# Gate logits from the transposed residual, and the dispatched rows written one step later, in a fused graph layer and mixture of experts

## What is computed

```python
# first layer
xn  = layernorm(x)
agg = eps * xn + einsum('bnm,bmd->bnd', adj, xn)
h   = silu(rmsnorm(agg @ W1 + b1) * rms_w)          # 512 features
x1  = x + h @ W2 + b2
# second layer, on u = layernorm(x1)
logits = u @ gate_w + gate_b                        # 16 experts
vals, idx = top_k(logits, 2);  w = softmax(vals)
expert_out[e] = relu(u @ w1[e] + b1[e]) @ w2[e] + b2[e]
y   = u + sum_k w[k] * expert_out[idx[k]]
out = x1 + layernorm(y) * gamma + beta
```

## Time and profile before

| | |
|---|---|
| median of 3 runs | 963.91 us (963.61 to 967.44) |
| the profiled execution | 964.82 us, its span 963.0 us |
| PE busy | 771.8 us (80%) |
| DVE busy | 598.9 us (62%) |
| ACT busy | 552.4 us (57%) |
| POOL busy | 508.1 us (53%) |
| HBM | 145 GB/s over the span |
| costliest group | L495 POOL, 256 indirect DMAs, 251.1 us busy |

### The profile page before, as it was taken

One profiled execution on the slowest core, in us unless ns is written; L12 is line 12 of the kernel. 1 busy time (PEld: TensorE's weight loads), 2 busy tenths in 40 slices (PEclk: granted clock), 3 DMA queues, 4 the chain that ended last, 5 costly groups with the idle time before them and its releaser, 6 DMA issues. The chain is left out here.

```text
span 963.0 us, 15762 instructions
## 1 busy us (share of the span) xinstructions
PE 771.8 (80%) x3649; PEld 506.7 (53%) x3650; DVE 598.9 (62%) x2164; ACT 552.4 (57%) x1123; POOL 508.1 (53%) x539
## 2 busy tenths in 40 slices
PE   5999999999999989858789999999986888772000
PEld 3455555555555445436567777777765666552000
DVE  2678787777777757764656665677755454443233
ACT  2799999999999969863223334545443433333121
POOL 2005666666666656666103555455455555557774
PEclk9999999999999989986989999999999978876555
DMA  5354444444344411142656777777775756553222
GB/s 158 112 209 144 150 148 147 150 146 149 133 146 148 139 54 48 43 112 80 180 149 168 184 187 196 200 218 211 215 194 166 193 145 169 168 143 110 73 82 79
DMA packets 136676, 140.76 MB, mean 146 GB/s; under 512 B 18323, under 2 KB 112291, under 8 KB 136358
## 3 DMA queue, kind: packets, MB, share of 16 engines
q1 hardware_dynamic: 117750, 102.67, 35.4%
q0 software_dynamic: 16384, 34.11, 12.6%
q10 hardware_dynamic: 2480, 3.34, 1.0%
HBM read 74.57 MB, written 65.49 MB: 145 GB/s over the span
## 5 line engine op out<-in xcount | busy, mean ns | idle before, releaser
L495 POOL DMA_INDIRECT dispatched<-rows,slot_i x256 | 251.1, 981 | 207.0 <-issue 132.0
L518 POOL DMA_INDIRECT work<-results,place x184 | 180.5, 981 | 188.1 <-issue 69.6
L825 ACT ACTIVATE hid<-bank,wts 128x256 f32<-128x256 f32 x286 | 120.1, 471 | 272.3 <-PE bank L665 270.6
L665 PE MATMUL bank<-tut,wts 128*128 128x256 f32 x572 | 162.1, 409 | 42.4 <-DVE tut L1221 37.4
L680 PE MATMUL bank<-w_all,hid 128*128 x1144 | 175.2, 299 | 0.0
L1243 DVE SCALAR_TENSOR_TENSOR tout<-bank,gate,tin 128x128 f32<-128x128 f32 x274 | 83.5, 347 | 124.5 <-PE bank L680 119.1
L680 PEld LDWEIGHTS bank<-w_all,hid 128*128 128x128 f32 x1144 | 147.2, 201 | 18.4 <-issue 2.7
L665 PEld LDWEIGHTS bank<-tut,wts 128*128 128x128 f32 x572 | 105.0, 205 | 56.1 <-DVE tut L1221 40.6
L544 PE MATMUL bank<-agg,w_sb 128*128 128x512 f32 x256 | 124.9, 610 | 0.0
L559 PE MATMUL bank<-work,w_sb 128*128 128x512 f32 x256 | 118.7, 607 | 3.8 <-ACT work L810 3.8
L518 POOL DMA_INDIRECT rows<-results,place x72 | 69.6, 967 | 49.8 <-issue 26.9
(11 more groups left out here) (190 smaller groups left out, 1031.4 us busy)
## 6 DMA issues: line engine op xcount, KB each, us to landing
tin<-dispatched SPq DMA_DIRECT2D x143, 132.0 KB, 2.8
wts<-in_w_exp SPq DMA_DIRECT2D x143, 129.0 KB
results<-tout SPq DMA_DIRECT2D x26, 704.0 KB, 3.1
results<-tout SPq DMA_DIRECT2D x137, 128.0 KB, 2.0
xs<-in_x SPq DMA_DIRECT2D x32, 256.0 KB, 2.7
adj_sb<-in_adj_t SPq DMA_DIRECT2D x32, 256.0 KB, 3.0
out<-agg SPq DMA_DIRECT2D x32, 256.0 KB, 2.7
dispatched<-rows,slot_i POOLq DMA_INDIRECT x256
```

The costliest lines, as they stand in the source:

```text
L495: nc.gpsimd.indirect_dma_start(dispatched, bass.IndirectOffsetOnAxis(slot_i[:, k, n:n + 1], 0), rows[:, k, n // TOPK, n % TOPK, :], None). ...
L518: nc.gpsimd.indirect_dma_start(moe_of(g)[:, n // TOPK, n % TOPK, :], None, results, bass.IndirectOffsetOnAxis(place[:, g, n:n + 1], 0)).th ...
L665: last = nc.tensor.matmul(hid_ps[n % 2][:, c * TILE:(c + 1) * TILE], wts[:, k, c * P:(c + 1) * P], tut[:, n % 2, :], start=True, stop=True)
L825: last = nc.scalar.activation(hid[:, n % 2, c, :], hid_ps[n % 2][:, c * TILE:(c + 1) * TILE], ACT.Relu, bias=wts[:, k, F + c:F + c + 1], s ...
```

## The change

- x is passed a second time, transposed (features, graphs, nodes), and SP loads it in each step for group t (256 KB) into `x1_t`, a ring of three.
- The second layer's output is no longer taken out of PSUM by ACT (o_t). DVE adds it, b2 and the transposed x in one operation into `x1_t`, after adj plus eps and ahead of the slots. PE transposes `x1_t` back, and DVE copies the result to x1 (it no longer adds).
- The logits come from `x1_t` with gate weights of which the mean over features was taken off (a matmul with ones and one DVE operation, once); the scale 1/sigma and the bias are put on by four small DVE operations in place of one. PE's transposes of rows and ACT's copy ut are gone.
- ACT writes `rows` of group t-3 instead of t-2, in the same place of its step. The gap goes through a tile of its own, `gaps`; `slot_i` has six buffers instead of three.
- In the last steps relu of tile 0 comes ahead of step 33 on ACT.

```diff
@@ sync, step
+                g = t
+                if has(i, g):
+                    if g >= RING:
+                        sp.wait_ge(lg_done, count(i, g - RING + 1))
+                    sp.dma_start(x1_t[:, g % RING].rearrange("p (j n) -> p j n", n=P),
+                                 x_t[:, bass.ds(count(i, g, GB), GB), :]).then_inc(xt_in[g % RING], 16)
@@ tensor, step
-                g = t - 2
-                if has(i, g):
-                    k = g % RING
-                    pe.wait_ge(u_done, count(i, g + 1))
-                    if g >= 1:
-                        pe.wait_ge(slote_done, count(i, g))
-                    for j in range(GB):
-                        last = nc.tensor.transpose(misc_ps[:, j * P:(j + 1) * P], rows[:, k, j, 0, 0:D],
-                                                   ident[:])
-                    last.then_inc(ut_done, 1)
                 g = t - 1
                 if has(i, g):
-                    pe.wait_ge(ot_out, count(i, g + 1))
+                    pe.wait_ge(x1t_done, count(i, g + 1))
                     for j in range(GB):
-                        last = nc.tensor.transpose(out_ps[:, j * D:(j + 1) * D], o_t[:, j * P:(j + 1) * P], ident[:])
+                        last = nc.tensor.transpose(out_ps[:, j * D:(j + 1) * D],
+                                                   x1_t[:, g % RING, j * P:(j + 1) * P], ident[:])
                     last.then_inc(out_done, 1)
...
                 g = t - 2
                 if has(i, g):
-                    pe.wait_ge(ut_out, count(i, g + 1))
+                    if g >= 1:
+                        pe.wait_ge(slote_done, count(i, g))
                     for j in range(GB):
-                        last = nc.tensor.matmul(misc_ps[:, j * E:(j + 1) * E], ut[:, j * P:(j + 1) * P],
-                                                gw2_sb[:], start=True, stop=True)
+                        last = nc.tensor.matmul(misc_ps[:, (GB + j) * E:(GB + j + 1) * E],
+                                                x1_t[:, g % RING, j * P:(j + 1) * P], gw2_sb[:],
+                                                start=True, stop=True)
                     last.then_inc(lg_done, 1)
@@ scalar, step
-                g = t - 2
+                g = t - 3
                 if has(i, g):
                     k = g % RING
...
                     last.then_inc(u_done, 1)
-                g = t - 1
-                if has(i, g):
-                    act.wait_ge(ot_done, count(i, g + 1))
-                    nc.scalar.activation(o_t[:], out_ps[:, :], ACT.Identity, bias=b2_sb[:, 0:1]).then_inc(ot_out, 1)
...
-                if ahead_of_ut is not None:
-                    ahead_of_ut()
-                g = t - 2
-                if has(i, g):
-                    act.wait_ge(ut_done, count(i, g + 1))
-                    nc.scalar.activation(ut[:], misc_ps[:, :], ACT.Copy).then_inc(ut_out, 1)
...
             step(None, NG)
-            step(None, NG + 1, ahead_of_ut=lambda: tile_step(None, 0))
+            tile_step(None, 0)
+            step(None, NG + 1)
@@ vector
+            def centre_gate():
+                dve.wait_ge(gsum_mm, 1)
+                dve.wait_ge(gw2_made, 1)
+                nc.vector.scalar_tensor_tensor(out=gw2_sb[:], in0=misc_ps[:, 2 * GB * E:(2 * GB + 1) * E],
+                                               scalar=-2.0 / D, in1=gw2_sb[:], op0=ALU.mult, op1=ALU.add)\
+                    .then_inc(gw2_made, 1)
@@ vector, step: routing of t-3
-                    nc.vector.tensor_tensor(lgs[:], misc_ps[:, 0:GB * E].rearrange("p (j e) -> p j e", e=E),
-                                            gb_sb[:, :].unsqueeze(1).broadcast_to([P, GB, E]), ALU.add)\
-                        .then_inc(lg_out, 1)
+                    dve.nop(nofuse=True)
+                    for j in range(GB):
+                        last = nc.vector.scalar_tensor_tensor(
+                            out=lgs[:, j, :], in0=misc_ps[:, (GB + j) * E:(GB + j + 1) * E],
+                            scalar=rs[:, 1, k, j:j + 1], in1=gb_sb[:], op0=ALU.mult, op1=ALU.add)
+                    last.then_inc(lg_out, 1)
@@ vector, step: between adj plus eps and the slots
+                g = t - 1
+                if has(i, g):
+                    k = g % RING
+                    dve.wait_ge(xt_in[k], count(i, g // RING + 1, 16, 1))
+                    dve.wait_ge(ot_done, count(i, g + 1))
+                    nc.vector.scalar_tensor_tensor(out=x1_t[:, k], in0=out_ps[:, :], scalar=b2_sb[:, 0:1],
+                                                   in1=x1_t[:, k], op0=ALU.add, op1=ALU.add).then_inc(x1t_done, 1)
@@ vector, step: slots, residual
-                    nc.vector.tensor_copy(slot_i[:, k, :], slot_f[:]).then_inc(slot_done, 1)
+                    if g >= 2 * RING:
+                        dve.wait_ge(u_done, count(i, g - RING + 1))
+                    nc.vector.tensor_copy(slot_i[:, g % (2 * RING), :], slot_f[:]).then_inc(slot_done, 1)
...
-                    nc.vector.tensor_tensor(x1, out_ps[:, :].rearrange("p (b d) -> p b d", d=D), x1,
-                                            ALU.add).then_inc(x1_done, 1)
+                    nc.vector.tensor_copy(x1, out_ps[:, :].rearrange("p (b d) -> p b d", d=D)).then_inc(x1_done, 1)
```

More of the change, by code:

```diff
@@ L45, with gnn_moe @@
 RMS_EPS = 1e-6
-def gnn_moe(nc, x, adj_t, eps, w1, b1, rms_w, w2, b2, gate_w, gate_b, w_exp, w2_exp, b2_exp, gamma, beta, out):
+def gnn_moe(nc, x, x_t, adj_t, eps, w1, b1, rms_w, w2, b2, gate_w, gate_b, w_exp, w2_exp, b2_exp, gamma, beta, out):
     fp32, bf16, i32, u32 = mybir.dt.float32, mybir.dt.bfloat16, mybir.dt.int32, mybir.dt.uint32
@@ L84, in gnn_moe @@
         b2_sb = sb("b2_sb", [P, 1])
-        o_t = sb("o_t", [P, GB * P])
+        x1_t = sb("x1_t", [P, RING, GB * P])
         b2e_sb = sb("b2e_sb", [E, D])
@@ L214, in gnn_moe @@
         ot_done = sem("ot_done")
-        ot_out = sem("ot_out")
+        x1t_done = sem("x1t_done")
+        xt_in = ring_of("xt_in", RING)
+        gsum_mm = sem("gsum_mm")
         h_done = sem("h_done")
@@ L495, in step @@
                         nc.gpsimd.indirect_dma_start(
-                            dispatched, bass.IndirectOffsetOnAxis(slot_i[:, k, n:n + 1], 0),
+                            dispatched, bass.IndirectOffsetOnAxis(slot_i[:, g % (2 * RING), n:n + 1], 0),
                             rows[:, k, n // TOPK, n % TOPK, :], None).then_inc(scattered[k], 16)
@@ L554, in step @@
                         pe.wait_ge(mid_in, 16 * 4)
+                        nc.tensor.matmul(misc_ps[:, 2 * GB * E:(2 * GB + 1) * E], ones_f[:], gw_sb[:],
+                                         start=True, stop=True).then_inc(gsum_mm, 1)
                     pe.wait_ge(s_done, count(i, HC * (g + 1), 1, RING * HC))
@@ L732, in _, with step @@
             act.wait_ge(eps_in, 32)
-            def step(i, t, ahead_of_ut=None):
+            def step(i, t):
                 g = t + 3
@@ L790, in step @@
                     last.then_inc(xn_done, 1)
-                if ahead_of_ut is not None:
-                    ahead_of_ut()
-                g = t - 2
-                if has(i, g):
-                    act.wait_ge(ut_done, count(i, g + 1))
-                    nc.scalar.activation(ut[:], misc_ps[:, :], ACT.Copy).then_inc(ut_out, 1)
                 def half_gap(g):
                     act.wait_ge(gap_done, count(i, g + 1))
-                    gap = rows[:, g % RING, :, :, D + 1:D + 2].rearrange("p j c o -> p (j c o)")
-                    nc.scalar.activation(gap, gap, ACT.Tanh, scale=0.5).then_inc(tanh_done, 1)
+                    nc.scalar.activation(rows[:, g % RING, :, :, D + 1:D + 2].rearrange("p j c o -> p (j c o)"),
+                                         gaps[:, g % 2].rearrange("p j c -> p (j c)"), ACT.Tanh, scale=0.5)\
+                        .then_inc(tanh_done, 1)
                 if not has(i, t) and has(i, t - 3):
@@ L1028, in step @@
                 if i is None and t == 2:
+                    centre_gate()
                     dve.wait_ge(b2_cut, 1)
@@ L1359 @@
         "x": a["x"].transpose(1, 0, 2),
+        "x_t": a["x"].transpose(2, 0, 1),
         "adj_t": a["adj"].transpose(2, 0, 1),
```

17 lines of the change are left out of this document (8 added, 9 removed).

## The result

The changed kernel is slower: 972.15 us (median of 22 runs, 968.25 to 983.53) against 965.99 for the kernel before in the same comparison (22 runs, 960.47 to 970.41). The ratio is 1.0075, with a 95% interval of 1.0059 to 1.0090. The forecast was a ratio of 0.996 and a range of 951 to 969; sign and range were both missed. Ratios leave out the few runs in which the chip was in a slower state; medians are over all runs.

What follows compares the result with a forecast made beforehand. The TensorE-VectorE ring (11.83 us) and GpSimd's slower scatter (about 12.2) were taken to pace the first stage. Terms: +4.8 to group 31's second layer, -8.2 at the stage's end, -0.5 after, -3.9; median 960.0 us, range 951 to 969.

Steps and rivals of the forecast that it cites:

- the ring: First stage: second layer, VectorE's slots to product, then TensorE's mean square and gate logits close each step in 11.83 us.
- The rival that the operation doesn't lengthen the steps: First stage: the ring shrinks elsewhere, steps stay at 12.17 us, total 951.6; chance 0.10.
- The size of the ring: 0.61 a step: Regular step: new VectorE operation 0.66 less 0.05, second layer ending before the rank matmul; ring grows to 12.44 us.
- Loop: Steps 3 to 24: 20 steps at 12.44 give +5.4 us, steps 3 and 4 +1.2; +6.6 together.
- Steps 25 and 26: Late first stage, now 31.85 us: 27.8, or 29.7 if the clock still drops; -4.0 or -2.1, -3.0 taken.
- Steps 27 to 29: Late first stage: +1.8 us for the three steps.
- The second layer of group 31: Near the first stage's end: 6.7 - 3.0 + 1.8 - 0.7, so 4.8 us later than 415.28.
- The end of the stage: Group 31's second layer to its slots: 31.2 us becomes 23 as logits need no rows; -8.2 us.
- Behind the slots: From group 31's slots to tile 12's load: as now, less some half clock, -0.5 us; tile 15 not late.
- The scatter rival: Loop: new loads slow scattering beyond 12.44 us a group, ScalarE still waits; at 12.7 about 969 us; chance 0.02.
- the end gives little back: Stage end: relu and merge of tile 0 come first at half clock; end gives only 1.5, total 967; chance 0.12.
- What would show it: Right: 12.4 us steps, TensorE waiting about 1.4, no landing wait. Wrong: steps at most 12.2, half clock between 30 and 330.

Runs made afterwards that it cites:

- before_add: The kernel before plus one unused 128x512 VectorE operation per step, ahead of the slots and waiting for the second layer: 977.41 us against 967.82, ratio 1.0101.
- after_filler: The changed kernel plus two unused 256-column TensorE matmuls in each step: 973.21 us, ratio 1.0087 to the kernel before.
- logits_tail_root: The changed kernel with early gate logits, idle matmuls in steps 32 to 34, and ScalarE's root of group 31 ahead of relu of tile 0: 945.47 us.
- logits_tail: The changed kernel with gate logits ahead of the mean square and unused matmuls in TensorE's waits of steps 32 to 34: 943.94 us, ratio 0.9786.
- double_add_filler: The changed kernel with the new add done twice and four unused 256-column matmuls per step: 992.13 us against 965.12 for the kernel before, ratio 1.0280.
- after: The changed kernel itself, against the kernel before: 972.15 us against 965.99, ratio 1.0075.
- double_add: The changed kernel with the new VectorE add done twice, second result unused: 1065.03 us, ratio 1.1004 to the kernel before.
- logits_first: The changed kernel with TensorE's gate logits moved ahead of the mean-square matmul: 946.16 us, ratio 0.9771 to the kernel before.

## Why the prediction was wrong, point by point

- *What bounds the kernel; the ring.* Right as a mechanism. The new operation waits for the second layer, TensorE waits for the product, ScalarE's wait for a landing is gone. The rival that the operation doesn't lengthen the steps fell (before_add: +9.6 us by itself).
- *The size of the ring: 0.61 a step.* Too small by 0.06. The "saving" of 0.05 (second layer done before the rank matmul) was real in before_add (12.42), and absent in the changed kernel (12.50), where the operation starts 0.11 behind the second layer's end (87.08 to 87.19). In 22 steps this is 1.3 to 1.5 us. One stretch of half clock at 207.4 us, behind a wait of 1.51, adds 1.9 in the profiled execution; the sum had no half clock in the loop. Loop: forecast +6.6, measured +10.3; start of step 3 forecast +0.1, measured -1.2.
- *Steps 25 and 26.* Forecast -3.0, measured -1.45: the clock still drops behind the early list (the lower of the two values worked out, -2.1, was nearly it), and the second layer there takes 4.13.
- *Steps 27 to 29.* Forecast +1.8, measured +5.3. Set against its size this is the term that failed most. It was taken as three regular steps at full clock; before_add, with the same ring, has +1.8 here (37.28 us where before has 35.48). In the changed kernel's trace two of the three run at half clock in part, at 364.4 behind a wait of 1.29, which costs 1.7, and at 402.0, which costs 1.5. The latter is behind a wait for the product that is 2.18 long:

```profile
401.82 1.94 PE L615 MATMUL bank<-prod,ones_f 128*128 128x512 f32 x2 [2.18 <-DVE prod L1137]
403.55 1.73 PE L630 MATMUL bank<-gw_sb,x_t 128*128 128x16 f32 x8
405.12 3.76 PE L550 MATMUL bank<-agg,w_sb 128*128 128x512 f32 x4
```

  In step 29 there is no aggregation any more (t+3 is past the last group), so its 0.95 us are added to the wait of 1.29. The prediction had the sum for this (it reckoned the wait at 1.4) and did not ask in which step the cover thins out. after_filler has no stretch in step 27, but still one in step 29 (399.4).
- *Steps 30 and 31.* Forecast -0.7, measured -0.4.
- *The second layer of group 31*: -1.2 + 10.3 - 1.45 + 5.3 - 0.4 = +12.5, where 4.8 was forecast. But for the start, each term is off to the same side.
- *The end of the stage.* From the second layer of group 31 to the end of its slots 25.8 us where before had 31.2: -5.4, forecast -8.2. The mechanism was right: TensorE no longer waits for rows. The step-by-step sum of the prediction came to 21.6 at full clock and 24.3 with half clock, and 23 was taken. In the trace it is half clock in full: from the first operation of group 30's slots (442.12) to tile 0's merge (448.38) are 6.3 us, where the prediction had 4.0 at full clock and logits_tail_root, which runs these matmuls at full clock, needs 3.9. Of the 2.8 us by which the term failed, 1.3 are this choice. The rest is on VectorE (start, us, [idle]):

```profile
428.31 0.36 DVE L976 TENSOR_SCALAR away<-upto_t 128x16 f32<-128x16 f32 x1
...
430.56 0.66 DVE L1042 SCALAR_TENSOR_TENSOR lgs<-bank,rs,gb_sb 128x16 f32<-128x16 f32 x4
...
442.04 0.16 DVE L1017 SCALAR_TENSOR_TENSOR nb<-bn,rs 128x4 f32<-128x4 f32 x1 [1.21 <-ACT rs L744]
```

  and it is seen in what TensorE waits for:

```profile
433.79 0.20 PE L577 MATMUL bank<-cnt,before 128*128 128x64 bf16 x1 [2.36 <-DVE carry L1078]
...
440.89 0.20 PE L577 MATMUL bank<-cnt,before 128*128 128x64 bf16 x1 [1.37 <-DVE carry L1078]
...
452.18 0.23 PE L577 MATMUL bank<-cnt,before 128*128 128x64 bf16 x1 [3.84 <-DVE carry L1078]
```

  A part of the early list (2.2 us from 428.31), and the four small logits operations (0.66, costed at nothing for the loop, where VectorE has 1.3 idle), stand in front of the routing there, where VectorE has nothing idle: group 29's slots are written 7.8 us behind the start of the second layer, where 7.1 was worked out. Group 31's root, behind relu of tile 0 on ScalarE, was counted at 0.4 and holds VectorE for 1.21; logits_tail and logits_tail_root put the price of this order at 1.0 us.
- *Behind the slots.* Forecast -0.5, measured +0.1 (7.1 at the slots' end, 7.3 at tile 12). Tile 15's load follows tile 12's at 12.7 us as before: scatters are not late, as forecast, though GpSimd's last issue is now at 478.45 instead of 464.55.
- *The sum* was of one sign by a narrow margin, a loss of 4.8 against a gain of 8.7, and every miss but the start's fell on the side of the loss. The steps that failed, forecast against measured: the loop (+6.6, +10.3), in which the ring was 0.06 too small and half clock was left out; steps 27 to 29 (+1.8, +5.3), in which half clock was left out; the end (-8.2, -5.4), in which half clock was taken at about half of what had been worked out, and VectorE's own work at 1.5 us too little; steps 25 and 26 (-3.0, -1.45). Together these are 11.5 us off, and 6.4 of them are half clock in this one execution (1.9 + 3.2 + 1.3); without these 6.4 the shift at tile 12 would be +0.9, no gain either. The medians moved by +6.2 and not by the +11.7 of the two profiled executions, so how much of the half clock most executions have stays open. The scatter rival's 969 for a pace of 12.7 is 968 by its own rule of 3 us for each 0.1, which changes nothing. The range reached to 969 by "the end gives little back"; it did not reach to a case in which the loop, the late steps and the end are each off by 1.5 to 4 us together. 12.5 - 5.4 + 0.1 = +7.2, or 7.3 without rounding, is what was measured at tile 12.
- *What would show it.* Steps of 12.4 with a wait of about 1.4 for the product came (12.50, 1.29). GpSimd waiting for tanh (L790) came too, in late groups 5.7 us at 361.56, 2.3 at 375.76 and 4.2 at 416.62; in the loop it waits for the slots (L1116, 4.0 us, 13 times between 100 and 330). Of the signs of being wrong one stretch of half clock came, at 207.4.

## What to carry to other kernels

When an operation is moved onto the chain that closes each step, it is paid in full, and a buffer that the move frees is worth nothing in the loop as long as the chain is slower than what the buffer decoupled. So make both one decision: first list the chain, and look for an operation between its last wait and the next step that needn't be there; here moving the gate logits, on top of the change, was worth 26 us, while the change alone cost 6. At the ends of a pipeline go through the steps one by one for what no longer runs beside a wait, and where the clock was at half before, price the matmuls there at half clock after.

## What the runs showed of the hardware that was not expected

- The granted clock in a loop that is otherwise busy went with a wait that recurs. Half clock between step 1 and step 27 was 3.4 us with a wait of 0.23 us a step (double_add_filler), 10.2 with 1.29 (after; 6.8 of them stand behind the early list, as before), and 133 with 1.95 (double_add), at a price of some 70 us. Useless matmuls in the wait gave nearly all of it back.
- The 128x512 operation out of PSUM takes 0.75 us by its own row, and the next instruction starts 0.67 behind its start; the ring pays 0.67. The Trainium skill, VectorE: DVE Perf Modes, section on the TRN2 errata, gives 0.66 by its figures, an estimate: the trace agrees with it as a pace, and its row is 0.09 longer.
- The same programs ran longer on two of the chips (986.51 and 983.40 against 965.12 to 967.82 for the kernel before; 974.62 against 946.16 for logits_first), in the traces with idle times of about 1.1 us in front of VectorE instructions that wait for nothing but their predecessor; the ratio of one kernel to another changes with it (0.9771 and 0.9903 for the same pair). Its cause stays open.
